# Graph network kernel: groups of 7x128 edges with windows of 32 nodes, and rings of six for gathered rows

## What is computed

```
x = layernorm(x + sage(x))       # 3 layers: msg = relu(x[src] + edge_attr_16 @ emb), mean over dst,
                                 #   then agg @ Wl + bl + x @ Wr (relu between layers)
x = layernorm(x + gin(x))        # 2 layers: msg = edge_weight * x[src], sum over dst, two products; then unit norm
x = layernorm(x + aggr(x))       # sum over dst of x[dst] * edge_attr_64
x = layernorm(x + gat(x))        # 3 attention layers with 8 heads of 8 features:
                                 #   h = x @ W.T; e = leaky_relu(a_s[src] + a_d[dst])
                                 #   alpha = exp(e - max over dst) / sum over dst; out = sum of alpha * h[src]
```

## Time and profile before

| | us |
|---|---|
| median of 3 runs | 17362.4 (17359.42 to 17365.91) |
| profiled execution, span from first to last instruction | 22236.9 |
| PE busy | 10574.4 (48%) |
| DVE busy | 6788.2 (31%) |
| ACT busy | 3759.7 (17%) |
| POOL busy | 12396.4 (56%) |

### The profile page before, as it was taken

One profiled execution on the slowest core, in us unless ns is written; L12 is line 12 of the kernel. 1 busy time (PEld: TensorE's weight loads), 2 busy tenths in 40 slices (PEclk: granted clock), 3 DMA queues, 4 the chain that ended last, 5 costly groups with the idle time before them and its releaser, 6 DMA issues. The chain is left out here.

```text
span 22236.9 us, 220022 instructions
## 1 busy us (share of the span) xinstructions
PE 10574.4 (48%) x59536; PEld 9523.6 (43%) x59537; DVE 6788.2 (31%) x17499; ACT 3759.7 (17%) x5833; POOL 12396.4 (56%) x12932
## 2 busy tenths in 40 slices
PE   5777744444444421112111155555655555655555
PEld 5666634443444411111111145555455555455554
DVE  1111111111111111111111155555555555555555
ACT  0000000000000000000000033333333333333333
POOL 4555456665666646665666635555455555455553
PEclk5555555555555555555555555555555555555555
DMA  2222111111111111111111112222122222122221
GB/s 47 46 46 47 40 26 27 27 27 25 27 27 27 27 20 23 23 23 23 23 23 23 23 45 57 56 57 56 48 56 56 55 56 56 49 56 56 55 56 41
DMA packets 1022298, 881.00 MB, mean 40 GB/s; under 512 B 725873, under 2 KB 727665, under 8 KB 1022235
## 3 DMA queue, kind: packets, MB, share of 16 engines
q0 software_dynamic: 413696, 444.31, 11.0%
q1 hardware_dynamic: 608539, 435.96, 6.7%
HBM read 865.07 MB, written 14.17 MB: 40 GB/s over the span
## 5 line engine op out<-in xcount | busy, mean ns | idle before, releaser
L626 POOL DMA_INDIRECT rows<-node_table,idx x6464 | 6188.8, 957 | 3914.5 <-issue 1961.1
L1262 POOL DMA_INDIRECT rows<-gat_table,idx x4848 | 4680.8, 966 | 4606.8 <-DVE msg L1458 2707.4
L655 PE MATMUL bank<-sel,msg 128*64 128x48 f32 x10720 | 1292.5, 308 | 4484.4 <-DVE msg L691 1961.8
L655 PEld LDWEIGHTS bank<-sel,msg 128*64 128x64 f32 x10720 | 1194.0, 224 | 4582.8 <-DVE accT L668 1747.8
L1293 PE MATMUL bank<-avm,bufB 48*128 48x16 f32 x9696 | 2098.4, 363 | 630.3 <-ACT avm L1339 453.9
L1293 PEld LDWEIGHTS bank<-avm,bufB 48*128 48x128 f32 x9696 | 2033.6, 316 | 694.7 <-ACT avm L1339 469.5
L1417 DVE CUSTOM_DVE_ANT_0 far<-scores,far 128x1024 f32<-128x1024 f32 x1818 | 2129.3, 1221 | 487.4 <-remote 420.7
L626 POOL DMA_INDIRECT rows<-in_x,idx x1616 | 1526.6, 945 | 1162.9 <-issue 529.6
L1348 ACT ACTIVATE far<-bufA,subcol 128x1024 f32<-128x1024 int32 x1818 | 2063.4, 1147 | 508.1 <-issue 244.8
L655 PE MATMUL scores<-sel,msg 128*64 128x48 f32 x5440 | 655.9, 308 | 2272.9 <-DVE msg L691 968.1
L668 DVE TENSOR_TENSOR accT<-accT,bank 64x48 f32 x670 | 131.9, 197 | 5104.8 <-remote 3997.3
(11 more groups left out here) (150 smaller groups left out, 11092.9 us busy)
## 6 DMA issues: line engine op xcount, KB each, us to landing
bufA<-in_dst_rows SPq DMA_DIRECT2D x606, 512.0 KB
rows<-node_table,idx POOLq DMA_INDIRECT x6464
rows<-gat_table,idx POOLq DMA_INDIRECT x4848
bufA<-in_attr SPq DMA_DIRECT2D x202, 256.0 KB
bufB<-in_attr SPq DMA_DIRECT2D x606, 64.0 KB
idx<-in_src SPq DMA_DIRECT2D x1616, 4.0 KB
rows<-in_x,idx POOLq DMA_INDIRECT x1616
node_table<-tbuf SPq DMA_DIRECT2D x52, 128.0 KB
```

The lines of the kernel that those rows point to most:

```text
L626: nc.gpsimd.indirect_dma_start(rows[s][:, j, 0:D], None, table, bass.IndirectOffsetOnAxis(idx[s][:, j:j + 1], 0)).then_inc(s_rows[s].handl ...
L655: last = nc.tensor.matmul(bank[3 + s][0:D, 0:WIN], msg[s][:, j, 0:D], sel[s][:, j, :], start=j == 0, stop=j == G - 1)
L1262: nc.gpsimd.indirect_dma_start(rows[s][:, j, :], None, gat_table, bass.IndirectOffsetOnAxis(idx[s][:, j:j + 1], 0)).then_inc(s_rows[s].han ...
```

## The change

Groups have 7 x 128 edges, so there are 231. Windows have 32 nodes, so two subwindows. A ring length `RR` = 6 is used in both kinds of pass for `rows` and `idx`; all other buffers have `R` = 3 slots and are indexed by `s % R`. Loop bodies hold six groups in all passes. In the attention pass, SP's load of `bufA` gets a wait for `far_ready`. POOL's wait for rows now looks six groups back. At the start, `dst_rows` is laid out as three parts of 77 groups.

```diff
-G = 8
+G = 7
-WIN = 48
+WIN = 32
 R = 3
-RG = 4
+RR = 6
...
-        idx = [sb(f"idx{i}", [P, G], I32) for i in range(RG)]
-        rows = [sb(f"rows{i}", [P, G, ROW]) for i in range(RG)]
-        bufA = [sb(f"bufA{i}", [P, GE]) for i in range(RG)]
...
-        far = [sb(f"far{i}", [P, GE]) for i in range(NSUB)]
+        idx = [sb(f"idx{i}", [P, G], I32) for i in range(RR)]
+        rows = [sb(f"rows{i}", [P, G, ROW]) for i in range(RR)]
+        bufA = [sb(f"bufA{i}", [P, GE]) for i in range(R)]
...
+        far = [sb(f"far{i}", [P, GE]) for i in range(R)]
...
-                ends = st[0:HALF, 0:2, 0:2]
-                for h in range(2):
+                ends = st[0:PART, 0:2, 0:PARTS]
+                for h in range(PARTS):
...
-        def turns(body, R=R):
-
-            for g in range(R):
+        def turns(body):
+
+            for g in range(RR):
                 body(g, g, 0)
 
             def rest(fori):
-                with fori(1, NG // R) as it:
-                    for s in range(R):
-                        body(it * R + s, s, it)
+                with fori(1, NG // RR) as it:
+                    for s in range(RR):
+                        body(it * RR + s, s, it)
...
+        def turn(s, it):
+
+            return it * (RR // R) + s // R
...
                         po.wait_ge(s_idx[s].handle, s_idx[s].at(it * 16 + 16))
-                        if due(g - R + 1):
-                            po.wait_ge(q["rows_free" if attr else "msg_ready"].handle, q["rows_free" if attr else "msg_ready"].at(g - R + 1))
+                        if due(g - RR + 1):
+                            po.wait_ge(q["rows_free" if attr else "msg_ready"].handle, q["rows_free" if attr else "msg_ready"].at(g - RR + 1))
...
-                        if due(g - RG + 1):
-                            sp.wait_ge(q["selT_ready"].handle, q["selT_ready"].at(g - RG + 1))
-                        sp.dma_start(bufA[s][:].bitcast(I32), A["dst_rows"][ds(g, 1), :].broadcast_to([P, GE])
-                                     ).then_inc(s_bA[s].handle, 16)
-                    turns(body, RG)(sp.Fori)
+                        if due(g - R + 1):
+                            sp.wait_ge(q["selT_ready"].handle, q["selT_ready"].at(g - R + 1))
+                            sp.sem_inc(s_passed.handle, 1)
+                            sp.wait_ge(q["far_ready"].handle, q["far_ready"].at(NSUB * (g - R + 1)))
+                        sp.dma_start(bufA[s % R][:].bitcast(I32), A["dst_rows"][ds(g, 1), :].broadcast_to([P, GE])
+                                     ).then_inc(s_bA[s % R].handle, 16)
+                    turns(body)(sp.Fori)
...
-                        if due(g - RG + 1):
-                            po.wait_ge(q["msg_ready"].handle, q["msg_ready"].at(g - RG + 1))
+                        if due(g - RR + 1):
+                            po.wait_ge(q["msg_ready"].handle, q["msg_ready"].at(g - RR + 1))
...
-                                out=far[k][:], in0=scores[:], in1=far[k][:], scale=1.0, scalar=-3.0e38, op0=ALU.subtract,
+                                out=far[k][:], in0=scores[:, 0:GE], in1=far[k][:], scale=1.0, scalar=-3.0e38, op0=ALU.subtract,
```

More of the change, by code:

```diff
@@ L41 @@
 SLOPE = 0.2
[L42 to L43 removed]
+PARTS = 3
+PART = NG // PARTS
+assert NG == PARTS * PART and RR % R == 0 and RR * (NG // RR) < NG and 2 * NG <= 512
 def ds(start, size):
@@ L592, in sum_pass @@
         def sum_pass(name, table, attr=False, aux=False):
-            s_rows = [sem(f"{name}_rows_loaded{i}") for i in range(R)]
+            s_rows = [sem(f"{name}_rows_loaded{i}") for i in range(RR)]
             with nc.Block() as block:
@@ L638, in body @@
                             for j in range(G):
-                                last = nc.tensor.matmul(bank[s][:, j * D:(j + 1) * D],
-                                                        bufB[s][0:EA, j * P:(j + 1) * P], emb[:], start=True, stop=True)
+                                last = nc.tensor.matmul(bank[s % R][:, j * D:(j + 1) * D],
+                                                        bufB[s % R][0:EA, j * P:(j + 1) * P], emb[:], start=True, stop=True)
                             last.then_inc(q["ea_ready"].handle, 1)
@@ L647, in body @@
                             for j in range(G):
-                                last = nc.tensor.matmul(bank[6][:, 0:WIN], bufA[s][:, j * P:(j + 1) * P], sel[s][:, j, :],
+                                last = nc.tensor.matmul(bank[6][:, 0:WIN], bufA[s % R][:, j * P:(j + 1) * P], sel[s % R][:, j, :],
                                                         start=j == 0, stop=j == G - 1)
@@ L654, in body @@
                         for j in range(G):
-                            last = nc.tensor.matmul(bank[3 + s][0:D, 0:WIN], msg[s][:, j, 0:D], sel[s][:, j, :],
+                            last = nc.tensor.matmul(bank[3 + s % R][0:D, 0:WIN], msg[s % R][:, j, 0:D], sel[s % R][:, j, :],
                                                     start=j == 0, stop=j == G - 1)
@@ L1222, in gat_pass @@
         def gat_pass(name):
-            s_rows = [sem(f"{name}_rows_loaded{i}") for i in range(RG)]
+            s_rows = [sem(f"{name}_rows_loaded{i}") for i in range(RR)]
             edge = bank[4]
@@ L1292, in values @@
                         for j in range(G):
-                            last = nc.tensor.matmul(edge[:, j * 2 * H:(j + 1) * 2 * H], bufB[s][0:WIN, j * P:(j + 1) * P],
+                            last = nc.tensor.matmul(edge[:, j * 2 * H:(j + 1) * 2 * H], bufB[s % R][0:WIN, j * P:(j + 1) * P],
                                                     avm[:], start=True, stop=True)
@@ L1300, in sums @@
                         for j in range(G):
-                            last = nc.tensor.matmul(wide[s % 2][0:ROW, 0:WIN], msg[s][:, j, :], sel[s][:, j, :],
+                            last = nc.tensor.matmul(wide[s % 2][0:ROW, 0:WIN], msg[s % R][:, j, :], sel[s % R][:, j, :],
                                                     start=j == 0, stop=j == G - 1)
@@ L1347, in distances @@
                                 ac.wait_ge(q["max_done"].handle, q["max_done"].at(NSUB * (g - 1) + k + 1))
-                            nc.scalar.activation(far[k][:], bufA[s][:].bitcast(I32), ACT.Square, bias=subcol[:, k:k + 1],
+                            nc.scalar.activation(far[k][:], bufA[s % R][:].bitcast(I32), ACT.Square, bias=subcol[:, k:k + 1],
                                                  scale=BIG).then_inc(q["far_ready"].handle, 1)
@@ L1450, in body @@
                         if real:
-                            ve.wait_ge(s_bA[s].handle, s_bA[s].at(it * 16 + 16))
-                            if due(g - RG + 1):
-                                ve.wait_ge(q["edge_ready"].handle, q["edge_ready"].at(g - RG + 1))
-                            nc.vector.tensor_scalar(bufB[s][0:WIN, :], bufA[s][0:WIN, :].bitcast(I32), first[0:WIN, ds(g, 1)], part[0:WIN, :],
+                            ve.wait_ge(s_bA[s % R].handle, s_bA[s % R].at(turn(s, it) * 16 + 16))
+                            if due(g - R + 1):
+                                ve.wait_ge(q["edge_ready"].handle, q["edge_ready"].at(g - R + 1))
+                            nc.vector.tensor_scalar(bufB[s % R][0:WIN, :], bufA[s % R][0:WIN, :].bitcast(I32), first[0:WIN, ds(g, 1)], part[0:WIN, :],
                                                     ALU.subtract, ALU.is_equal).then_inc(q["selT_ready"].handle, 1)
@@ L1486, in _ @@
                     n2 = link.close()
-                    for g in range(3, RG):
+                    for g in range(3, RR):
                         link.offset = n1 + n2 * (g - 2)
```

155 lines of the change are left out of this document (79 added, 76 removed).

## The result

The changed kernel takes 17412.75 us (median of 7 runs, 17411.98 to 17418.33), the kernel before 17362.4 us beside it (7 runs, 17359.4 to 17365.91). The ratio is 1.003, 95% interval 1.002 to 1.004: **slower, by 50 us**. Forecast were 17352 us and no change that can be told.

The account below looks back on a forecast made before the run. The prediction took POOL's back-to-back gathers as the bound. From 17362.4 us, +10 (gathers), -10 and -2 (ends of passes), +2 (start) and -10 (lengthened gathers) gave 17352 us, no change that can be told, range 17325 to 17395.

Parts of the forecast that it names:

- The bound: Whole timed kernel: POOL's 12928 gathers one after another at 1.2477 us each, with recorded stalls belonging to the recording.
- Lengthened gathers, -10 us: Gathers that start beside DVE's `sel`: shorter `sel` lengthens them less, net between -20 and +5, taken as -10 us.
- 47 us left under the median: Median 17362.4 us less stretches and gather pace, 17315 us: the room for stalls and lengthened gathers.
- Rings, 0 us: Rows and index lists in rings of six remove stalls: between 0 and -47 us when timed, taken as 0.
- rival 3: Loop bodies of six groups are fetched again each turn, stopping POOL: 633 us more, 17990 us, chance 0.06.
- Start, +2 us: Ahead of the first gather: reductions over three thirds instead of two halves, +2 us, between 0 and 4.
- Eight gathers, +10: All passes together: 231 groups of 7 need eight more gathers at 1.2477 us, +10 us.
- Ends of passes, -12: Pipeline drains after a pass's last gather get shorter: -10 us over three attention passes, -2 us over five sum passes.
- Maxima 1.07 us: DVE's maxima in an attention group: three of 1.22 us become two of about 1.07 us.
- The record's own span, 20500 to 21700: Profiled execution, outside the timed forecast: POOL's sum-pass waits fall by more than half, span 20500 to 21700 us.
- 1 and 2: Rivals: stalls are real, 16800 us, chance 0.10; 47 us or dense stretches hide some stalls, 17280 us, chance 0.17.
- 3 and 4: Rivals: loops refetched, 17990 us, chance 0.06; PE period or smaller rings miss POOL's pace, 17430 us, chance 0.07.

Follow-up runs that it names:

- experiment 2: Changed kernel with groups of 8, windows of 48 and two parts again, keeping rings and loops of six: 17418.14 us, 1.003 of the kernel before.
- experiment 5: Kernel before's rings and loops with groups of 7, windows of 32 and three parts: 17430.24 us, 1.0021 of the kernel before.
- experiment 7: Changed kernel with one operand each of `sel`, `bufB` and `msg` in PSUM in the attention passes: 17300.27 us, 0.9945 of the kernel before.
- experiment 3: Changed kernel with rings and loop bodies of three everywhere, groups of 7 and windows of 32 kept: 20537.19 us, 1.1826 of the kernel before.
- experiment 4: Changed kernel with windows of 48 (three subwindows) and groups of 7: 17502.29 us, 1.0078 of the kernel before.

## Why the prediction was wrong, step by step

*The bound: right.* POOL's pace holds both kernels; inside a pass nothing else parts the gathers. (The median is 22% under the profiled span; the 28% of the prediction is the span over the median. Nothing rests on it.) That the stalls are no part of the timed kernel was right for the chips that timed it, but the reason given, that recording makes them, is refuted: two chips have them unrecorded.

*Lengthened gathers, -10 us: the step that failed. Measured +53.7.* I summed the durations of `sel` and took a share. But `sel`, `bufB` and `msg` together last the same in the attention passes before and after (1257.8 and 1252.9 us), and gathers lose 107.7 us to them before and 143.3 after: what counts is where operations fall against the gathers' 1.25 us beat, not how long they are together. The parts don't add up either. In attention, rings of six alone take the 107.7 to 140.0 (experiment 2), groups of 7 alone to 153.9 (experiment 5), and both to 143.3; in the sum passes the 10.3 go to 11.8, 8.9 and 28.4 (22.5 when recorded again). So the sign could not be had from a sum of durations, and that it came out as a loss is a matter of where the operations happened to fall. For attention experiment 7 and the table under experiment 5 show that it is these three operations and no others. For the sum passes there is no such experiment: the count says only that 22.5 of the 28.4 us lie in gathers that start inside `sel`, `msg` or `far`. I also bounded the effect by "47 us left under the median", and that bound was false: the nine stretches are 1110 us, not 1185.5, which leaves 122 us, nearly the 118.0 that the rows of before now show.

*Rings, 0 us: wrong too, by +15.1* (stretches of 1024.0 us for the 1008.9 of experiment 5; with the -0.8 that experiment 5 has to before, the 14.3 of the table). GpSimd's `DRAIN` at the end of a pass ends 8.65 us after the last gather instead of some 4.5, and in the sum passes the block's end waits for it; 13.1 us of the 15.1 are that wait. The prediction has no term for it. Its, read as a jump to code not at hand, show a block's end as well, and no instruction packet moved there. Of rival 3 the first sign came (231 packets for 37), on VectorE, where the prediction said it would hide; and it hid.

*Start, +2 us: measured -27.1.* I costed the reductions and not how the transfer's shape holds SyncE; the trace that the prediction used has the long issue as well (20.05 us).

*Eight gathers, +10: right. Ends of passes, -12: overrated.* They drain behind no backlog; with groups of 7 alone (experiment 5) the three stretches behind attention passes are 3.9 us shorter (381.5 to 377.7), the five behind sum passes 3.1 us longer (628.2 to 631.3).

*Maxima 1.07 us: 1.09, right.*

*The record's own span, 20500 to 21700, POOL's waits halved: not tested as such;* on the chips with stalls the kernel nearest to it takes 23166 and 23327 us, as lists come late. I had seen that a list is issued behind the other load and called the added wait covered by 26 us; with stalls of 10 us and more it isn't.

*Rivals.* 1 and 2 did not come, nor did 3 and 4. Rings of three for everything would have cost 18% (experiment 3), which the change avoids by its six for rows. None of the four was a gather held by VectorE, which made the sign. The errors partly cancel: +63.7 us for lengthened gathers, +15.1 for rings, +11.2 for ends of passes and -29.1 for the start are 60.9, and the median is 60.4 over the forecast.

## What to carry to other kernels

Where GpSimd issues gathers back to back, an account of the span (stretches without gathers, count times pace, busy time above the floor of one gather) tells within 1 us where a change went. Where gathers are seen to be longer beside VectorE operations that read only SBUF, as `sel`, `bufB` and `msg` do, give these an operand in PSUM: in the attention passes this ended all of the lengthening, 0.6% of the time here, even where the operation itself became 43% longer. Until then the lengthening depends on where operations fall, so a change of group size or ring moves the time by that alone, here by 32 to 46 us in the attention passes. Before trusting the stalls of a record, hold its span against the timed median: if they differ, the record here told durations of single instructions, not waits, and not the idle stretches either (1185.5 us for 1110.45).

## What the hardware showed that I had not expected

- A transfer onto 101 partitions makes SyncE's next issue take 19.85 us, where 77 or 96 + 5 take 0.4.
- A gather that starts inside `bufB` or `msg` ends 0.37 us late when that operation ends 0.49 us after the gather's start, and one into which `bufB` begins after 0.31 us ends 0.30 us late.
- GpSimd's `DRAIN` behind its last gather ends 8.65 us after it with rings and loops of six, 4.65 with three. It is seen only where the other engines are done sooner.
- A VectorE loop of six groups was fetched anew at each turn in one of three passes with the same body, 2.9 us in the turn shown, and not in the two others; with windows of 48 (experiment 4) in none, with groups of 8 (experiment 2) in two.
- Chips differ: before takes 17362 to 17366 us in three of the sets of runs, 17395 on one chip, 22198 and 22203 on two; the changed kernel, 1.003 of before on the first, is at 1.05 and 1.04 on the last two in the form nearest to it, with the `msg` operand in PSUM.
